# Row numbers of the last graph layer's gathers, made beside the load of the features

## What is computed

```python
edge_index = jnp.stack([src, dst])
x = x + _L0_gnn_ref(_layernorm(x, axis=-1), edge_index, ...)
x = x + _L0_ffn_ref(_layernorm(x, axis=-1)[None], ...)[0]
...
x = x + _L3_gnn_ref(_layernorm(x, axis=-1), edge_index, L3_gnn_weight, L3_gnn_attn_l, L3_gnn_attn_r)
x = x + _L3_ffn_ref(_layernorm(x, axis=-1)[None], L3_ffn_gate_w, L3_ffn_gate_b, ...)[0]
```

```python
xt = jnp.matmul(x, weight).reshape(-1, heads, out_ch)
row, col = (edge_index[0], edge_index[1])
alpha_l = jnp.einsum('ehd,hd->eh', xt[row], attn_l)
alpha_r = jnp.einsum('ehd,hd->eh', xt[col], attn_r)
alpha = jax.nn.softmax(jax.nn.leaky_relu(alpha_l + alpha_r, 0.01), axis=1)
tmp = jnp.einsum('nh,nhd->nd', alpha[:n], xt[col[:n]])
```

## Time and profile before

| | us |
|---|---|
| median of 3 runs | 11839.42 |
| lowest and highest | 11832.27 and 11841.63 |
| the profiled execution, its span | 11863.4 |

### The profile page before, as it was taken

The page is one execution under the profiler, slowest core; times in us unless marked ns, Lnnn a source line. Parts: engine busy times, 40 slices in busy tenths (PEclk is TensorE's granted clock), DMA queues, the critical chain, the costliest instruction groups (busy, mean ns, idle before and its releaser), DMA issues. The chain is left out here.

```text
span 11863.4 us, 161789 instructions
## 1 busy us (share of the span) xinstructions
PE 7067.3 (60%) x37393; PEld 5112.1 (43%) x37394; DVE 6591.0 (56%) x17647; ACT 2681.0 (23%) x6652; POOL 7275.8 (61%) x7041
## 2 busy tenths in 40 slices
PE   2234266666688225844555488884774777646395
PEld 1111144444444124622333366663663555434284
DVE  8763178888888531133444488884124777724413
ACT  0002011111233132120000233333222444322322
POOL 0676777777688767767777777774313777151510
PEclk9667688888899658977776578776887888678597
DMA  5101166666544205532333011111554333355253
GB/s 151 54 11 51 36 198 203 208 205 204 156 134 135 63 17 158 169 99 79 102 102 87 14 9 9 9 9 27 186 179 124 104 104 104 89 166 162 67 183 129
DMA packets 872265, 1274.59 MB, mean 107 GB/s; under 512 B 216773, under 2 KB 651631, under 8 KB 871053
## 3 DMA queue, kind: packets, MB, share of 16 engines
q1 hardware_dynamic: 568684, 719.17, 19.2%
q0 software_dynamic: 303136, 550.30, 17.8%
HBM read 972.38 MB, written 303.22 MB: 108 GB/s over the span
## 5 line engine op out<-in xcount | busy, mean ns | idle before, releaser
L2966 POOL DMA_INDIRECT gat_edges_rows<-gat_table,gat_src x1080 | 1089.0, 1008 | 329.5 <-issue 323.7
L1829 DVE TENSOR_TENSOR l_acc<-l_acc,l_sum_o 128x260 f32 (+1 forms) x1664 | 702.0, 422 | 681.5 <-PE l_sum_o L1746 567.7
L2641 POOL DMA_INDIRECT m_by_node<-m_ffn_ys,m_ffn_home x392 | 387.6, 989 | 969.4 <-issue 887.3
L1332 POOL DMA_INDIRECT l_sum_rows<-l_feats,l_sum_ix x832 | 817.1, 982 | 264.1 <-issue 219.2
L1746 PE MATMUL l_sum_o<-l_sum_rows,l_sum_s 128*128 128x256 f32 x1664 | 615.3, 534 | 586.1 <-DMA l_sum_rows<-l_feats,l_sum_ix 554.2
L1332 POOL DMA_INDIRECT l_max_rows<-pairs,l_max_ix x832 | 804.6, 967 | 254.2 <-issue 244.2
L1478 PE MATMUL l_max_qe<-l_acc,l_max_st 128*128 x1664 | 579.2, 508 | 550.6 <-DVE l_max_prod L1533 549.5
L2678 PE MATMUL m_ffn_hp<-m_ffn_xt,m_ffn_w1b 128*128 128x256 f32 x3200 | 755.7, 391 | 60.2 <-DVE m_ffn_xt L2715 58.5
L3133 DVE TENSOR_REDUCE gat_edges_top<-gat_edges_mx 128x4 f32<-128x512 f32 x1080 | 733.5, 683 | 64.4 <-PE gat_edges_mx L3037 62.4
L2688 PE MATMUL m_ffn_yp<-m_ffn_w2b,m_ffn_ht 128*128 128x256 f32 x3200 | 741.5, 385 | 44.9 <-ACT m_ffn_ht L2705 43.2
L1746 PEld LDWEIGHTS l_sum_o<-l_sum_rows,l_sum_s 128*128 128x128 f32 x1664 | 424.2, 267 | 777.5 <-issue 599.9
(11 more groups left out here) (737 smaller groups left out, 18999.8 us busy)
## 6 DMA issues: line engine op xcount, KB each, us to landing
along<-l_max_rows SPq DMA_DIRECT2D x208, 512.0 KB, 2.9
l_sum_rows<-along SPq DMA_DIRECT2D x208, 512.0 KB, 3.3
m_ffn_w1b<-in_L_ffn_W SPq DMA_DIRECT2D x108, 512.0 KB, 4.2
m_ffn_w2b<-in_L_ffn_W SPq DMA_DIRECT2D x108, 512.0 KB, 3.9
m_ffn_xs<-sorted_rows SPq DMA_DIRECT2D x196, 257.0 KB, 3.8
m_ffn_w1b<-in_L_ffn_w SPq DMA_DIRECT2D x32, 1024.0 KB, 4.7
m_ffn_w2b<-in_L_ffn_w SPq DMA_DIRECT2D x32, 1024.0 KB, 5.3
l_proj_taken<-m_by_node SPq DMA_DIRECT2D x42, 768.0 KB, 7.3
```

The lines of the kernel that those rows point to most:

```text
L1332: pool.indirect_dma_start(rows[:, j, :], None, table, bass.IndirectOffsetOnAxis(ap=ix[:, j:j + 1], axis=0)).then_inc(sem, 16)
L1829: dve.tensor_tensor(a, a, o[:, j, 0:R].unsqueeze(1), ALU.add).then_inc(acc_own, 1)
L2966: pool.indirect_dma_start(rows[:, q % RR, j, :], None, table, bass.IndirectOffsetOnAxis(ap=L.src[:, t:t + 1], axis=0)).then_inc(got[q % GS ...
```

## The change

The four DMAs, the memset, the two casts and the two transposes leave `m3_proj` and stand in `load_x`. Their result goes into a new buffer `ends` of `Core`, 392 bytes of each partition, which is kept through the whole program. In `load_x` the four DMAs stand on SP between the load of tiles 0 to 47 and that of the last tile. The gathers read `core.ends` and wait for nothing but free buffers. `load_x` has four semaphores more (six), `m3_proj` five fewer (29 for 34). No arithmetic is added or dropped.

```diff
@@ MixFront
-        self.listed_rows = ph.sb("listed_rows", [T, 2, P], I32)
-        self.listed_f = ph.sb("listed_f", [T, 2, P])
-        self.ix = ph.sb("ix", [P, 2, T], I32)
-        self.turned = ph.ps("turned", [P, 2, T])
...
     def gathers(self, pool):
         bound = pool.to_reg(N - 1)
-        pool.wait_ge(self.staged, 1)
         for c in range(T // CH):
...
-                                        bass.IndirectOffsetOnAxis(ap=self.ix[:, 0, t:t + 1], axis=0),
+                                        bass.IndirectOffsetOnAxis(ap=self.core.ends[:, 0, t:t + 1], axis=0),
...
@@ load_x
             @block.vector
             def _(dve):
                 dve.memset(core.x[:, T - 1, :], 0.0).then_inc(zeroed, 1)
+                dve.memset(listed_rows[:], 0).then_inc(cleared, 1)
+                dve.wait_ge(listed, 64)
+                dve.tensor_copy(listed_f[:], listed_rows[:]).then_inc(as_f, 1)
+                dve.wait_ge(flipped_done, 1)
+                dve.tensor_copy(core.ends[:], flipped[:])
+
+            @block.tensor
+            def _(pe):
+                pe.wait_ge(as_f, 1)
+                for k in range(2):
+                    ins = pe.transpose(flipped[:, k, :], listed_f[:, k, :], core.ident[0:T, 0:T])
+                ins.then_inc(flipped_done, 1)
 
             @block.sync
             def _(sp):
                 sp.dma_start(core.x[:, 0:T - 1, :], x[0:(T - 1) * P, :].rearrange("(t p) d -> p t d", p=P)).then_inc(got, 16)
+                sp.wait_ge(cleared, 1)
+                for k, v in enumerate((dst_d, src_d)):
+                    sp.dma_start(listed_rows[0:T - 1, k, :], v[0:(T - 1) * P].rearrange("(t p) -> t p", p=P)
+                                 ).then_inc(listed, 16)
+                    sp.dma_start(listed_rows[T - 1:T, k, 0:LAST], v[(T - 1) * P:N].rearrange("(o p) -> o p", o=1)
+                                 ).then_inc(listed, 16)
                 sp.wait_ge(zeroed, 1)
                 sp.dma_start(core.x[0:LAST, T - 1, :], x[(T - 1) * P:N, :]).then_inc(got, 16)
```

More of the change, by code:

```diff
@@ L889, in room @@
         self.mixed = ph.sb("mixed", [P, 2, CH, C])
-        (self.zeroed, self.listed, self.as_f, self.turned_done, self.staged, self.taken, self.own, self.ready, self.done,
-         self.joined, self.folded, self.added) = [
-            ph.sem(n) for n in ("zeroed", "listed", "as_f", "turned_done", "staged", "taken", "own", "ready", "done",
-                                "joined", "folded", "mix_added")]
+        (self.taken, self.own, self.ready, self.done, self.joined, self.folded, self.added) = [
+            ph.sem(n) for n in ("taken", "own", "ready", "done", "joined", "folded", "mix_added")]
         self.got = [ph.gathered_sem(k) for k in range(3)]
-    def load(self, sp, c):
-        if c:
-            return
-        sp.wait_ge(self.zeroed, 1)
-        for k, v in enumerate((self.dst_d, self.src_d)):
-            sp.dma_start(self.listed_rows[0:T - 1, k, :], v[0:(T - 1) * P].rearrange("(t p) -> t p", p=P)
-                         ).then_inc(self.listed, 16)
-            sp.dma_start(self.listed_rows[T - 1:T, k, 0:LAST], v[(T - 1) * P:N].rearrange("(o p) -> o p", o=1)
-                         ).then_inc(self.listed, 16)
-    def before(self, dve):
-        dve.memset(self.listed_rows[:], 0).then_inc(self.zeroed, 1)
-        dve.wait_ge(self.listed, 64)
-        dve.tensor_copy(self.listed_f[:], self.listed_rows[:]).then_inc(self.as_f, 1)
-        dve.wait_ge(self.turned_done, 1)
-        dve.tensor_copy(self.ix[:], self.turned[:]).then_inc(self.staged, 1)
-    def turns(self, pe):
-        pe.wait_ge(self.as_f, 1)
-        for k in range(2):
-            ins = pe.transpose(self.turned[:, k, :], self.listed_f[:, k, :], self.core.ident[0:T, 0:T])
-        ins.then_inc(self.turned_done, 1)
     def gathers(self, pool):
         bound = pool.to_reg(N - 1)
-        pool.wait_ge(self.staged, 1)
         for c in range(T // CH):
@@ L2276, in __init__, with load_x @@
         self.weight = [sb(f"weight{k}", [P, T, 2]) for k in range(4)]
-def load_x(nc, core, x):
+        self.ends = sb("ends_of_firsts", [P, 2, T], I32)
+def load_x(nc, core, x, src_d, dst_d):
     with Phase(nc, "load_x") as ph:
-        zeroed, got = ph.sem("zeroed"), ph.sem("got")
+        listed_rows = ph.sb("listed_rows", [T, 2, P], I32)
+        listed_f = ph.sb("listed_f", [T, 2, P])
+        flipped = ph.ps("flipped", [P, 2, T])
+        zeroed, got, cleared, listed, as_f, flipped_done = [ph.sem(k) for k in (
+            "zeroed", "got", "cleared", "listed", "as_f", "flipped_done")]
         with nc.Block() as block:
@@ L3383, in layer2_gnn, with layer3_gnn @@
     return SoftmaxFront(acc, own_part, park)
-def layer3_gnn(nc, core, src_d, dst_d, w, front):
+def layer3_gnn(nc, core, w, front):
     H, C = 4, D // 4
@@ L3396, in layer3_gnn @@
                        (1, w["attn_r"].rearrange("(o h) e -> o (h e)", o=1))], front=front)
-    return MixFront(table, left, src_d, dst_d, H)
+    return MixFront(table, left, H)
 LAYERS = ("L0_gnn_", "L0_ffn_", "L1_gnn_", "L1_ffn_", "L2_gnn_", "L2_ffn_", "L3_gnn_", "L3_ffn_")
```

10 lines of the change are left out of this document (5 added, 5 removed).

## The result

The changed kernel takes 11811.9 us (median of 13 runs, 11792.6 to 11818.5), the kernel before beside it 11839.4 (13 runs, 11830.8 to 11852.8). The ratio is 0.9975, 95% interval 0.9967 to 0.9983: 27.6 us less, faster by 0.25%. A gain of this size had a chance of 0.02. But the steps that it costed came out within 0.2 us. The gain came from a phase that the change doesn't touch.

What follows compares the result with a forecast made beforehand. Phases never overlap, and POOL's gathers were taken to set `m3_proj`. The terms -3.83 - 0.32 + 0.25 + 0.2 + 0 gave -3.7 us, from 11839.4 to 11835.7 us; range 11826 to 11848.

Steps and rivals of the forecast that it cites:

- Start of the gathers: In `m3_proj`, POOL's first gather starts 0.86 us behind the phase's start, 3.83 us earlier than before.
- the semaphores: POOL clears semaphores one by one between phases: five fewer in `m3_proj` give -0.32 us, four more in `load_x` +0.25.
- `load_x`, +0.45: `count_main` starts at 27.3 instead of 26.83: +0.2 us for the lists in the rings, +0.25 for semaphore clears.
- The chain of casts: Cast, transposes and cast, 1.09 us, moved to `load_x` beside the last tile's transfer: 0 us, up to 1.1 if uncovered.
- the forecast's sign: In `load_x` after the change, DVE's last cast ends before the last packets of the features.
- the code fetch: Rival in `m3_proj`: POOL must first fetch its code, leaving the sum at -2.4 or +0.1 us; chance 0.12.
- the held-up tile: Rival in `load_x`: the lists delay the last tile, +1.1 us overall; chance 0.04, or 0.12 with a milder case.
- `m0_put` and `m1_put` keep their lengths: Sign: these phases, 137.10 and 137.13 us before, stay as long; a move of some us would mean placement is at work.
- The place of everything else: Rival in nearly all phases: buffers 416 bytes further on, later code shifted; 12 us or more either way, chance 0.08.

Runs made afterwards that it cites:

- f0_before: The kernel before, unchanged, run again for a second profile: 11848.3 us, ratio 0.9996.
- f3_after: The changed kernel, run again for a second profile, beside the kernel before: 11820.8 us, ratio 0.9975.
- f1_place: The kernel before with one unused buffer of 392 bytes, so that buffers stand as in the changed kernel: 11855.5 us, ratio 1.0002.
- h1_dve3: The kernel before with three tiny idle DVE memsets at the end of `load_x`, nothing else moved: 11822.5 us, ratio 0.9970.
- h2_act: The changed kernel with the moved memset on POOL and both casts on ACT instead of DVE: 11867.6 us, ratio 1.0008.
- h3_after100: The changed kernel with 97 more idle DVE memsets in `load_x`: 11859.8 us, ratio 0.9997.
- i3_after31: The changed kernel with 28 more idle DVE memsets in `load_x`: 11831.8 us, ratio 0.9969.
- i2_wait4: The changed kernel with two more DVE semaphore instructions (four waits already reached) ahead of each one-hot of `l0_sum`: 11801.7 us, ratio 0.9942.

## Why the prediction was wrong

By its own steps:

- **Start of the gathers, 3.83 us.** Right. The first gather came 0.81 us behind ACT's first instruction against the forecast 0.86; with the semaphores the sum had 4.15 for the phase, and 3.98 was measured in the profile after, 4.2 between `f0_before` and `f3_after`.
- **`load_x`, +0.45.** Right: 27.28 against 26.83, and between `f0_before` and `f3_after` 0.41 (26.90 and 27.31). The terms came out too: the last packet 0.18 later, the time behind it 0.27 longer. The chain of casts costs nothing, as put, but not for the reason given: in the first profile its end, 25.90, is 0.15 behind the last packet, so the forecast's sign, a cast that ends before the packets, fails there and holds only in `f3_after`. What covers it is the 1.5 us between the last packet and the next phase. The rivals of the code fetch and of the held-up tile are refuted by the same rows: the gather starts within 0.9 us of ACT, and `count_main` far before 30.98.
- **`m0_put` and `m1_put` keep their lengths.** Right, and no comfort. After:

```profile
4372.71 0.19 ACT L2550 COPY m_put_ix<-m_put 128x2 int32<-128x2 int32 x1 [16.93 <-PEq L65]
...
4509.70 0.32 SPq L238 DMA_DIRECT2D m_ffn_carried<-gat_unmoved  x1
```

  136.99 us, against 137.10.
- **The place of everything else, chance 0.08.** This is the step that failed. The rival named two things, buffers 416 bytes further on and later code a few instructions further. I then argued about the first alone: the earlier trace rows compare two phases with different buffer places. They say nothing on code, and the second half of the rival was left without a row, a size or a chance of its own. The first half was indeed nothing (`f1_place`, 1.0002). The second was the 30 us (`h1_dve3`). The forecast took it as granted that a phase whose instructions and operands are unchanged keeps its length. `h1_dve3` and `h2_act` show that this is false here. For the gathers of `m3_proj` the prediction did ask whether they meet the same DVE instructions as before; for the phases that the change leaves alone it did not.
- **The size.** What could have been read from the trace of before: `l0_sum` ends with more than 100 us in which only POOL works, its 536 moves take 1.42 us on average where an undisturbed one takes 0.96, and 17 of them fit a turn of DVE's loop, with nearly the same pattern in each turn. An engine that sets the end and is locked to another's rhythm changes by whole steps. 208 quads are 26 turns, some 24 of them inside the loop; with one move more in each, 24 moves fewer are left for the tail, where each takes 0.96 + 0.30 = 1.26 us: 30 us. 29 to 30 was measured. That the gap lies at a fixed place of the code, and that three instructions would move it the good way, could not be read from one trace; it took the experiments. I had costed no such step, in either direction; a range with that step would have reached some 30 us to both sides.

In short: the sum of the costed terms was -3.7, and the touched phases gave -3.5. The median moved by -27.6 because DVE's loop in `l0_sum` stands three instructions further on in its code. The gain doesn't belong to the change: `h1_dve3` has it without the change, `h2_act` and `h3_after100` have the change without it.

## What to carry to other kernels

Where an engine that sets the end of a phase is locked to the rhythm of another (durations that come in two or three fixed values, the same pattern each turn), give every edit ahead of that loop a chance to move it by a whole step, in either direction, and say how large the step is. Before a gain of a few tenths of a per cent is put down to an edit, compare the phases that it doesn't touch, and run the kernel before with as many idle instructions as the edit adds. And such a lock can be worked on directly: two cheap instructions per quad delayed DVE by 0.2 us in each, freed POOL, and brought 30 us more on top of the shifted loop. Three brought less, since DVE, by then the engine that sets the end, pays for each.

## What the runs showed of the hardware

- In a loop DVE's stream of instructions has gaps of 0.10 to 0.12 us at fixed places of its code, 128 instructions apart. From the kernel before, 3 instructions more ahead of the loop move it from instruction 186 of the turn to 183 (`f3_after`), 31 more to 155 (`i3_after31`), and with 100 more it is at 214 = 86 + 128 (`h3_after100`).
- A move of POOL (an indirect DMA of 128 records out of SBUF) takes 0.96 us alone. Caught behind a DVE operation that reads two operands in SBUF, it ends 0.83 to 0.87 us after that operation, in the ordinary quads with a total of 1.4 (one-hot) or 1.8 to 2.0 us (weighing). It is caught if it starts 0.05 us or more behind the operation's start. Up to 0.03 us behind it gets through in 0.96, and DVE's one-hot beside it takes 0.73 (`f3_after`) or 0.77 us (`i2_wait4`) where it takes 0.69. DVE's adds, which read one operand in PSUM, didn't hold it up: the move at 3321.77 in `f3_after` lies over one and took 0.95.
- A shift of nearly all buffers by 416 bytes in each partition changed nothing that could be measured (`f1_place`, ratio 1.0002, interval 0.9993 to 1.0012).
- Chips differ: on two of them every kernel took about 14800 us instead of 11840, and `l0_sum` 1269 to 1487 us where it takes 873 to 937 on the others.
